# The rotation's products on halves of the TensorE array, two token tiles side by side

## What is computed

```python
U, _ = jnp.linalg.qr(P)              # (288, 64)
R = expm(skew(silu(cond) @ W.T + b)) # (32, 64, 64), one for each sequence
z = jnp.einsum('btn,nd->btd', x, U)
z_rot = jnp.einsum('btd,bde->bte', z, R)
x_rot = x + jnp.einsum('btd,nd->btn', z_rot - z, U)
```

## Time and profile before

| | us |
|---|---|
| median of 3 runs | 4510.08 |
| the profiled execution | 4508.88 |
| its span, first to last instruction | 4507.2 |
| TensorE busy | 4177.3 (93%) |
| VectorE busy | 3633.4 (81%) |
| ScalarE busy | 2300.9 (51%) |
| GpSimd busy | 1113.7 (25%) |

### The profile page before, as it was taken

The page is one execution under the profiler, slowest core; times in us unless marked ns, Lnnn a source line. Parts: engine busy times, 40 slices in busy tenths (PEclk is TensorE's granted clock), DMA queues, the critical chain, the costliest instruction groups (busy, mean ns, idle before and its releaser), DMA issues. The chain is left out here.

```text
span 4507.2 us, 124159 instructions
## 1 busy us (share of the span) xinstructions
PE 4177.3 (93%) x46073; PEld 3554.6 (79%) x46073; DVE 3633.4 (81%) x7651; ACT 2300.9 (51%) x3892; POOL 1113.7 (25%) x2051
## 2 busy tenths in 40 slices
PE   6764899999999999999999999999999999999998
PEld 4653788888888888888888888887888888888886
DVE  5775888898888997777777777789888888888885
ACT  1212555555555555555555555555555555555553
POOL 1102222222222233222222222233222222222212
PEclk8576999999999999999999999999999999999999
DMA  3101111101111111111110111111010111101010
GB/s 80 23 1 55 30 28 31 31 25 31 27 31 29 27 46 54 30 31 29 30 31 25 31 28 31 32 46 49 23 31 24 29 28 25 28 25 28 25 26 20
DMA packets 122213, 141.80 MB, mean 31 GB/s; under 512 B 14414, under 2 KB 117748, under 8 KB 122080
## 3 DMA queue, kind: packets, MB, share of 16 engines
q1 hardware_dynamic: 121936, 139.75, 11.8%
q10 hardware_dynamic: 144, 0.22, 0.0%
HBM read 110.87 MB, written 29.06 MB: 31 GB/s over the span
## 5 line engine op out<-in xcount | busy, mean ns | idle before, releaser
L1023 DVE TENSOR_REDUCE mx<-S 128x4 f32<-128x1024 f32 x768 | 903.0, 1217 | 174.3 <-PE S L1265 166.8
L758 ACT ACTIVATE pT<-S 128x1024 f32<-128x1024 f32 x768 | 745.5, 1023 | 369.1 <-PE S L1293 369.0
L706 ACT ACTIVATE hf<-M 128x512 f32<-128x512 f32 (+1 forms) x480 | 267.0, 556 | 736.9 <-DVE hl L1014 389.0
L620 POOL TENSOR_SCALAR hh<-hf 128x512 fp32r<-128x512 f32 (+1 forms) x480 | 282.0, 588 | 830.8 <-ACT hf L706 781.8
L1293 PE MATMUL S<-qT,kT 32*128 32x256 f32 x9216 | 425.1, 295 | 17.0 <-ACT pT L758 13.9
L1306 PE MATMUL A<-pT,V 128*32 128x256 f32 x6144 | 412.8, 386 | 25.1 <-ACT pT L758 25.1
L1293 PEld LDWEIGHTS S<-qT,kT 32*128 32x128 f32 x9216 | 328.6, 184 | 87.9 <-issue 46.9
L1200 PE MATMUL A<-wqkv_hi,xh 128*128 128x288 f32 x1152 | 283.6, 328 | 92.8 <-DVE x L1070 90.1
L1345 PE MATMUL M<-xh,w_hi 128*128 128x256 f32 x1728 | 364.2, 292 | 1.2 <-POOL xh L594 1.2
L1384 PE MATMUL M<-w_lo,hh 128*128 128x288 f32 x1728 | 353.0, 304 | 0.0
L1345 PE MATMUL M<-xh,w_lo 128*128 128x256 f32 x1728 | 344.4, 280 | 0.0
(11 more groups left out here) (245 smaller groups left out, 9862.0 us busy)
## 6 DMA issues: line engine op xcount, KB each, us to landing
mid<-xbo SPq DMA_DIRECT2D x64, 288.0 KB, 4.0
xld<-mid SPq DMA_DIRECT2D x64, 288.0 KB, 3.7
xa<-mid SPq DMA_DIRECT2D x64, 288.0 KB, 3.6
gA<-gates SPq DMA_DIRECT2D x96, 144.0 KB, 3.3
gM<-gates SPq DMA_DIRECT2D x96, 144.0 KB, 3.6
xld<-in_x_dram SPq DMA_DIRECT2D x32, 288.0 KB, 3.8
xa<-in_x_dram SPq DMA_DIRECT2D x32, 288.0 KB, 3.5
out_dram<-xbo SPq DMA_DIRECT2D x32, 288.0 KB, 2.2
```

What stands on the lines that cost most here:

```text
L620: pool.tensor_scalar(hh[:, 2 * f:2 * f + m, :].rearrange("p m c -> p (m c)"), hf[:, f % 3, 0:m * T], 1.0, 0.0, ALU.mult, ALU.add).then_inc ...
L706: act.activation(hf[:, f % 3, 0:c], MBANK[f % 2][:, 0:c], gelu(n)).then_inc(s["m_hf"], 1)
L758: act.activation(pT[:, g % 2, 2 * h:2 * h + 2, :], S[:, 2 * h:2 * h + 2, :], ACT.Exp, scale=float(HD) ** -0.5).then_inc(s["a_ex"], 1)
L1023: dve.tensor_reduce(mx[:, p, :, :], S[:, r:r + 2, :].rearrange("p a (t k) -> p a t k", t=NT), AX.X, ALU.max).then_inc(s["a_mx"], 1)
```

## The change

R_z's product of 256 token columns becomes two of 128, one for each token tile, on the left and on the right 64 columns of the array, so that the result lies on partitions 0 to 63 for the first tile and 64 to 127 for the second. `zT` and `yT` become 128x128 with the same layout, and the two copies on ScalarE are of that shape. R_y becomes two products of 64x64 weights on the diagonal quarters of the array, with `eb` held on both partition halves, which takes a second DMA for each sequence. R_out's two products take their operands from the lower and the upper partition half, with `UT` held on both; the upper copy is made by ScalarE at the end of the preamble, beside VectorE's one. `U` stays as it is.

```diff
--- before.py
+++ after.py
@@ -50,7 +50,7 @@
     a_pr=2, a_prd=2, a_xa=16, a_x1=2, a_warm=2,
     m_g=16, m_bn=2, m_st=1, m_ve=1, m_rs=1, m_xn=2, m_gb=1, m_xb=1, m_xT=2, m_xf=3, m_xh=3, m_xl=1, m_h=5,
     m_hf=5, m_hh=5, m_hl=5, m_y=2, m_x2=2, m_out=16, m_mod=1, a_mod=1,
-    r_e=16, r_T=2, r_x=2, r_z=1, r_zs=1, r_y=1, r_ys=1, r_o=2, r_x3=2,
+    r_e=32, r_T=2, r_x=2, r_z=1, r_zs=1, r_y=1, r_ys=1, r_o=2, r_x3=2,
 )
 
 
@@ -87,7 +87,7 @@
         ident = sb("ident", [P, P])
         modT = sb("modT", [P, LAYERS, 12, B])
         U = sb("U", [KP, KC, ROT])
-        UT = sb("UT", [ROT, D])
+        UT = sb("UT", [P, D])
         mhalf = sb("mhalf", [P, 2])
         low_rows = sb("low_rows", [P, 1])
 
@@ -172,9 +172,9 @@
         rsM = sb("rsM", [P, NT])
         veM = sb("veM", [P, NT])
 
-        eb = sb("eb", [ROT, ROT])
-        zT = sb("zT", [ROT, T])
-        yT = sb("yT", [ROT, T])
+        eb = sb("eb", [P, ROT])
+        zT = sb("zT", [P, P])
+        yT = sb("yT", [P, P])
 
         w_in = sem("w_in")
         w_hi = sem("w_hi")
@@ -468,7 +468,8 @@
 
             def load_e(n):
                 wait(sp, "r_y", local(n), 0)
-                sp.dma_start(eb[:, :], expm[local(n)]).then_inc(s["r_e"], 16)
+                for h in range(2):
+                    sp.dma_start(eb[h * ROT:(h + 1) * ROT, :], expm[local(n)]).then_inc(s["r_e"], 16)
 
             def store(n):
                 if rot(n):
@@ -776,11 +777,11 @@
 
             def R_z(n):
                 wait(act, "r_z", local(n), 1)
-                act.activation(zT[:, :], MBANK[0][0:ROT, 0:T], ACT.Identity).then_inc(s["r_zs"], 1)
+                act.activation(zT[:, :], MBANK[0][:, 0:P], ACT.Identity).then_inc(s["r_zs"], 1)
 
             def R_y(n):
                 wait(act, "r_y", local(n), 1)
-                act.activation(yT[:, :], MBANK[0][0:ROT, 0:T], ACT.Identity).then_inc(s["r_ys"], 1)
+                act.activation(yT[:, :], MBANK[0][:, 0:P], ACT.Identity).then_inc(s["r_ys"], 1)
 
             def slot(a, m, d, p, nxt):
                 if a is None and p is None and nxt is not None:
@@ -1403,22 +1404,28 @@
 
                 wait(pe, "r_x", local(n), 2)
                 for k in range(KC):
-                    op = pe.matmul(MBANK[0][0:ROT, 0:T], U[:, k, :], xf[0:KP, k, :], start=(k == 0), stop=(k == KC - 1))
+                    for i in range(NT):
+                        op = pe.matmul(MBANK[0][i * ROT:(i + 1) * ROT, 0:P], U[:, k, :], xf[0:KP, k, i * P:(i + 1) * P],
+                                       start=(k == 0), stop=(k == KC - 1), tile_position=(0, i * ROT))
                 op.then_inc(s["r_z"], 1)
 
             def R_y(n):
 
                 wait(pe, "r_zs", local(n), 1)
-                wait(pe, "r_e", local(n), 16)
+                wait(pe, "r_e", local(n), 32)
                 constant_wait(pe)
-                pe.matmul(MBANK[0][0:ROT, 0:T], eb[:, :], zT[:, :], start=True, stop=True).then_inc(s["r_y"], 1)
+                for i in range(NT):
+                    rows = slice(i * ROT, (i + 1) * ROT)
+                    op = pe.matmul(MBANK[0][rows, 0:P], eb[rows, :], zT[rows, :], start=True, stop=True)
+                op.then_inc(s["r_y"], 1)
 
             def R_out(n, p):
                 wait(pe, "r_ys", local(n), 1)
                 if p is not None:
                     wait(pe, "a_mx", p, PAIRS - 1)
                 for i in range(NT):
-                    pe.matmul(S[:, i, 0:D], yT[:, i * P:(i + 1) * P], UT[:, :], start=True, stop=True).then_inc(s["r_o"], 1)
+                    rows = slice(i * ROT, (i + 1) * ROT)
+                    pe.matmul(S[:, i, 0:D], yT[rows, :], UT[rows, :], start=True, stop=True).then_inc(s["r_o"], 1)
 
             def new_weights(n, count):
 
@@ -1720,6 +1727,8 @@
                 length2(j + SQUARE_FROM)
             act.wait_ge(g_step, GS * ROT)
             act.activation(junk2[:, :], G[:, :], ACT.Square, accum_out=n2[:, :]).then_inc(u_n2, 1)
+            act.wait_ge(g_step, GS * ROT + 3)
+            act.activation(UT[ROT:P, :], G[0:ROT, :], ACT.Identity, scale=q[0][0:ROT, :])
 
         @block.vector
         def _(dve):
@@ -1834,7 +1843,7 @@
             dve.wait_ge(g_step, end + 2)
             dve.scalar_tensor_tensor(out=q[0][0:ROT, :], in0=dot[0:ROT, :], scalar=-1.0, in1=rt[0:ROT, :], op0=ALU.mult, op1=ALU.mult).then_inc(g_step, 1)
             dve.wait_ge(g_step, end + 3)
-            dve.tensor_scalar(UT[:, :], G[0:ROT, :], q[0][0:ROT, :], None, ALU.mult).then_inc(g_step, 1)
+            dve.tensor_scalar(UT[0:ROT, :], G[0:ROT, :], q[0][0:ROT, :], None, ALU.mult).then_inc(g_step, 1)
             dve.wait_ge(u_mm, 2)
             dve.tensor_copy(U[:, :, :], ABANK[0][0:KP, 0:KC * ROT].rearrange("p (k e) -> p k e", k=KC)).then_inc(g_step, 1)
 
@@ -1915,7 +1924,7 @@
             pe.matmul(ABANK[1][:, 0:ROT], house_row[:, :], sg[:, :], start=True, stop=True).then_inc(u_mm, 1)
             pe.wait_ge(g_step, GS * ROT + 4)
             for k in range(KC):
-                op = pe.transpose(ABANK[0][0:KP, k * ROT:(k + 1) * ROT], UT[:, k * KP:(k + 1) * KP], ident[0:ROT, 0:ROT])
+                op = pe.transpose(ABANK[0][0:KP, k * ROT:(k + 1) * ROT], UT[0:ROT, k * KP:(k + 1) * KP], ident[0:ROT, 0:ROT])
             op.then_inc(u_mm, 1)
```

## The result

The kernel after takes 4481.49 us (median of 5 runs, 4479.91 to 4484.44) against 4510.08 for the kernel before (5 runs, 4502.52 to 4513.9): a ratio of 0.9939, 95% interval 0.9925 to 0.9954. It is faster, by 28.6 us where 19.5 were forecast; the time lies in the range and 9 us under its likeliest value. The profiled executions took 4479.91 and 4508.88.

What follows compares the result with a forecast made beforehand. A loop through VectorE, then TensorE alone, was taken to bound each slot. Savings of 0.02 + 0.21 + 0.11 + 0.15 = 0.49 us times 28 (13.7) plus 5.8 give 19.5: 4490.5 us, by itself 4484 to 4498, range 4479 to 4503.

Steps and rivals of the forecast that it cites:

- VectorE gets it all back: Rival: GpSimd relief of 0.4 or more, TensorE's own saving counts, 0.77 us a slot: 4482.5 us; chance 0.10.
- VectorE was not the bound: Sign that the forecast is wrong: a full slot of 43.9 us or less.
- The clock's rival: Rival: shorter products leave TensorE idle and the granted clock drops once a slot: slower, 4538 us; chance 0.05.
- The halves run together: Changed products on TensorE: records on the two array halves overlap, so a full halving of their steps was taken.
- R_z is worth 0 to 0.1 in a full slot, ScalarE's `qk` is late next: R_z, 0.65 us shorter, gains only TensorE's lateness against ScalarE, taken 0.02 a slot; then `qk` is late.
- R_y 0.21: R_y, between qkv and down products in the loop: two steps of 0.11 less, 0.21 us a slot.
- R_out, "VectorE's loop passes it by", 0.11: R_out, 0.48 us shorter on TensorE, gains only 0.11 a slot, through VectorE's second add waiting less.
- The wait of 0.4 us forecast at 4139: TensorE's lead from R_out, 0.37 us, handed back as a wait for VectorE's low parts of k before the scores.
- The relief of GpSimd, 0.15: GpSimd's copies of V come earlier and overlap VectorE's `xl<-hf,xh` less: net 0.15 us a slot, bounds -0.3 and 0.5.
- zT, yT, the second load of the matrix, UT's second copy: ScalarE's smaller copies, the second `expm` load and the extra UT copy: nothing in a full slot.
- The end, 5.8: The last four slots, without qkv, where R_z counts too and the very last runs at half clock: 5.8 us together.

Runs made afterwards that it cites:

- `rz_back`: The kernel after with R_z as it was (one product of 256 columns) and two ScalarE copies into `zT`: slot 44.04 us, 4490.29 us (one run).
- `copy_first_after`: The kernel after with ScalarE's copy of qkv(0) moved ahead of the second `R_x` and the table load: slot 43.38 us, 4466.73 us, ratio 0.9914.
- `late_signal`: The kernel after, with VectorE told of R_out's second output only behind the second down product that follows: slot 44.01 us, 4483.22 us.
- `pe_less_early`: The kernel after without four of 27 terms of the first down product, right behind R_out, in the third layer: slot 43.48 us, 4466.07 us.
- `both_first`: The kernel before, with VectorE waiting for both outputs of R_out ahead of its first add: slot 44.71 us, 4507.19 us.
- `copy_first_before`: The kernel before with ScalarE's copy of qkv(0) moved ahead of the second `R_x` and the table load: slot 44.70 us, 4502.25 us.

## Why the prediction was right or wrong

The time lies in the stated range, but beyond the 4484 that the forecast allowed by itself; it was the widening towards the next rival that took it in. What that rival held, TensorE's own saving counted in full, is what happened, and I had given it a chance of 0.10. My sign that "VectorE was not the bound", a slot of 43.9 or less, was set too low: the slot took 44.00, the sign would have stayed silent, and VectorE was not the bound of that stretch. The clock's rival did not come: the grant stayed at 1.00 in the full slots. Some 3 us of the gain came ahead of the first rotation and up to 3 by the clock at the end, so the distance of 9 us to the forecast holds luck as well; the slot doesn't.

- *The halves run together*: right. R_z's twelve records take 0.88 us, R_y 0.36, R_out 0.69, as forecast (0.85, 0.36, 0.68).
- *R_z is worth 0 to 0.1 in a full slot, ScalarE's `qk` is late next*: right, 0.03 by `rz_back`, and the wait of 0.54 is there. `copy_first_after` shows that it was the cause: without it, 0.65 count.
- *R_y 0.21*: right, 0.20.
- *R_out, "VectorE's loop passes it by", 0.11*: the step that failed; it measured 0.47. A loop over VectorE and TensorE there is, but the stretch from R_out to the last transposes belongs to TensorE and not to VectorE. I had closed TensorE's half of the loop at the scores at 4139 alone, and let VectorE run on its own from R_x3 to kT, though the second `rden` waits for TensorE in every slot. The group row shows no idle time in brackets, since the wait stands inside it; the length of the row does, 0.55 for two of 0.26 that overlap when nothing holds them. The wait of 0.4 us forecast at 4139 did not come: it would have needed VectorE to stay where it was.
- *The relief of GpSimd, 0.15*: wrong as a term. `xl<-hf,xh` went from 1.19 to 1.15 only. The slowing itself is real, but it works as a buffer: VectorE loses some 0.5 us there when early (1.15 to 1.25) and gets it back when late (0.69 in `late_signal` and `pe_less_early`), so it hands VectorE's own small gains and losses back. That GpSimd's copies are its cause is read from what overlaps with what; no run took the copies away.
- *zT, yT, the second load of the matrix, UT's second copy*: nothing in a full slot, as forecast; no row of theirs stands in TensorE's waits, and the three parts measured alone fill the 0.70. The UT copy and the first load fall into the early part, which scatters by more than they could cost.
- *The end, 5.8*: 6.5 between the two profiled executions, 3.3 to 3.8 against the two whose grant did not fall from the 29th to the 30th R_y. The agreement of 6.5 with 5.8 is in part luck. The forecast priced the last rotation at half speed on both sides, as the kernel before had it (R_y's row 1.08 us); in `both_first` and `copy_first_before` that R_y took 0.61, at full speed, and in the kernel after 0.69, where its others take 0.44. So that term depends on the execution. What each product is worth in the last slots was not measured.
- *The rival "VectorE gets it all back"* came to within 1 us of the time with its 0.77 a slot, where 0.70 was measured. Its sum, TensorE's own saving in full, is what happened; its reason, a relief of 0.4 or more, is not. The meeting within 1 us is luck, for the early part and the end added their own.

## What to carry to other kernels

A row of the time line that merges several instructions can hide a wait: compare its length with the same row where nothing waits, before an engine is called free of the other. When two engines meet several times in a period, ask for each meeting which one came last; a saving counts in full if it lies on the late side up to the next meeting. And where a shortened step leaves a wait behind it, look at what the releasing engine does first: here moving one copy ahead of a table load nearly doubled what the change was worth in a slot (0.70 to 1.32 us).

## What the runs showed of the hardware

- *Two row halves in one bank.* R_y's two halves use different rows and different columns of the array and write the same bank, on different partitions. In one slot of after the single records start at 4136.049 and 4136.056, then at 4136.209 and 4136.216, each pair 7 ns apart, and the change of R_y alone moved the slot by 0.20 us. The Trainium skill (TensorEngine Tiling (Array Packing), Restrictions and Gotchas) says that different row tiles can't access one PSUM bank simultaneously; here they overlap (0.36 us to the next product, against 0.57 for the one product before), so for this shape the trace disagrees.
- *A waiting instruction holds up more than itself.* From the start of the pair of adds to the instruction behind it VectorE took 1.10 (before) and 1.07 us (`late_signal`) where the second add had to wait, and 0.74 where it had not. The pair of adds itself was longer by 0.12 and 0.10, so another 0.23 to 0.24 us lie behind it. In `both_first`, with the wait ahead of both adds, that time was 0.74 too. What VectorE's sequencer does there, the loop's end and its branches, is argued, not shown.
- *GpSimd beside VectorE.* One and the same VectorE operation, 128x512 from two SBUF tiles, took 0.69 us alone and 1.07 to 1.25 with GpSimd's copies of V under it, the same in every full slot of a kernel to 0.04 us.
- *The early part and the end scatter.* With identical instructions up to there, the first R_y came between 3167.55 and 3171.96 us. The end scatters as well, 126.03 to 129.18 us from the 28th R_y on with the same products, with the granted clock. A difference of 3 us between single executions of this kernel means nothing; the length of a slot, told to 0.01 us, does.
